# A three-layer graph attention kernel: every product of its loops made at least 65 rows and columns wide, and one tile's weighting moved from GpSimd to VectorE

## What is computed

```python
# layers 0 and 1 (4 heads, then 1), each with a further self loop on every node
xW = x @ W
e = leaky_relu(alpha_s[src] + alpha_d[dst], 0.2)
w = exp(e - segment_max(e, dst)[dst])
out = segment_sum(xW[src] * (w / segment_sum(w, dst)[dst]), dst) + bias
# elu between them; behind layer 1: x = layernorm(x + out)

# layer 2 (8 heads): edge features join the score
enc = relu(edge_attr @ edge_W.T + edge_b)
alpha = (h_src * a_src).sum() + (h_dst * a_dst).sum() + (enc * h_dst).sum()   # per head
# leaky_relu, softmax over the edges of a destination, weighted sum, + bias, residual, layernorm
```

## Time and profile before

| what | value |
|---|---|
| median of 3 runs | 2092.96 us (2092.95 to 2096.61) |
| the profiled execution | 2100.78 us, span 2099.0 us |
| TensorE busy | 1673.1 us, 80% of the span |
| VectorE busy | 1574.9 us, 75% |
| GpSimd busy | 1504.7 us, 72% |
| ScalarE busy | 1370.3 us, 65% |
| mean granted clock of TensorE | 0.824 |

### The profile page before, as it was taken

How to read it: one execution, slowest core, us unless ns; L and a number is a source line. 1 busy time by engine, 2 the same in 40 slices (tenths; PEclk the granted TensorE clock), 3 DMA queues, 4 the chain that set the end, 5 groups by cost and what they waited for, 6 DMA issues and landing times. The chain is left out here.

```text
span 2099.0 us, 43225 instructions
## 1 busy us (share of the span) xinstructions
PE 1673.1 (80%) x9241; PEld 1064.7 (51%) x9241; DVE 1574.9 (75%) x4409; ACT 1370.3 (65%) x5004; POOL 1504.7 (72%) x1648
## 2 busy tenths in 40 slices
PE   7377778777876577878878877789999999999984
PEld 5244445545544344545545444445565655565652
DVE  5567877777778456666656667879899998899997
ACT  3267776777675444545545446668888888888886
POOL 3677777777767577777777773667777777777873
PEclk9578877888787767777777787779999999999995
DMA  7655554555641344444444641434444444444431
GB/s 195 173 161 143 145 143 139 142 144 167 186 116 37 118 129 135 134 129 135 137 129 134 197 121 39 122 109 125 125 129 130 127 130 127 125 128 133 137 90 61
DMA packets 130636, 274.39 MB, mean 131 GB/s; under 512 B 39701, under 2 KB 65274, under 8 KB 130367
## 3 DMA queue, kind: packets, MB, share of 16 engines
q0 software_dynamic: 64128, 181.33, 32.1%
q1 hardware_dynamic: 61564, 86.45, 13.5%
q10 hardware_dynamic: 4699, 3.86, 0.7%
HBM read 255.00 MB, written 17.20 MB: 130 GB/s over the span
## 5 line engine op out<-in xcount | busy, mean ns | idle before, releaser
L1283 POOL DMA_INDIRECT rows<-table,index_all x1100 | 1073.7, 976 | 402.9 <-issue 304.9
L1801 PE MATMUL bank<-rows,onehot 128*128 128x264 f32 (+1 forms) x2200 | 863.2, 492 | 55.0 <-DVE rows L843 17.4
L854 DVE TENSOR_TENSOR sums<-sums,bank 128x264 f32 (+1 forms) x1320 | 556.8, 422 | 325.6 <-PE bank L1801 252.5
L1498 ACT ACTIVATE rows<-rows,wgt 128x33 f32<-128x33 f32 (+2 forms) x2740 | 706.3, 338 | 2.1 <-issue 1.1
L1801 PEld LDWEIGHTS bank<-rows,onehot 128*128 128x128 f32 x2200 | 416.7, 230 | 126.1 <-issue 77.7
L1721 PE MATMUL bank<-identb,onehotT 128*128 128x128 bf16 x1320 | 228.9, 261 | 41.9 <-issue 28.9
L1283 POOL DMA_INDIRECT late<-table,index_all x220 | 214.1, 973 | 67.0 <-issue 62.2
L1721 PEld LDWEIGHTS bank<-identb,onehotT 128*128 128x128 bf16 x1320 | 135.1, 117 | 155.0 <-issue 93.6
L1506 ACT ACTIVATE prod<-bank 128x512 f32<-128x512 f32 x240 | 134.1, 559 | 107.2 <-PE bank L1813 97.0
L1820 PE MATMUL bank<-late,onehotT 128*128 x1320 | 201.0, 290 | 1.3 <-DVE prod L863 1.3
L1450 ACT CAST onehot<-bank 128x768 f32<-128x768 bf16 x240 | 174.5, 729 | 40.5 <-PE bank L1721 40.3
(11 more groups left out here) (215 smaller groups left out, 2242.2 us busy)
## 6 DMA issues: line engine op xcount, KB each, us to landing
locb<-loc_d SPq DMA_DIRECT2D x120, 352.0 KB, 3.8
rows<-table,index_all POOLq DMA_INDIRECT x1100
flags<-flags_d SPq DMA_DIRECT2D x508, 27.5 KB
late<-table,index_all POOLq DMA_INDIRECT x220
table<-rows SPq DMA_DIRECT2D x25, 136.0 KB, 1.8
table<-rows SPq DMA_DIRECT2D x25, 134.0 KB, 2.7
late<-table SPq DMA_DIRECT2D x1, 3300.0 KB
table<-rows SPq DMA_DIRECT2D x25, 129.5 KB, 2.3
```

Of the source, the lines that this page charges most:

```text
L854: done(v.tensor_tensor(a, a, sum_bank(l, t, s)[:, 0:VV], ALU.add), "add")
L1283: g.indirect_dma_start(out=rows_of(l, t)[:, s, 0:ROW[l]], out_offset=None, in_=table[l], in_offset=bass.IndirectOffsetOnAxis(ap=index_all[ ...
L1498: i = a.activation(r, r, ACT.Copy, scale=wgt[:, t.u, h * B + s:h * B + s + 1])
L1801: done(m.matmul(sum_bank(l, t, s)[:, 0:VV], onehot[:, t.u, s, :], rows_of(l, t)[:, s, 0:VV], start=True, stop=True), "agg")
```

## The change

Every product of the loops gets a stationary operand of at least 65 rows and 65 columns. Operands that stood on few partitions (`runs`, `linkrow`, `scale`, `carry`, `edgew3`, `attrT`) get all 128, with zeros, or values that meet zeros, in the added ones. `scoresT`, `weightsT` and the ends' transposes take all 88 lines in each layer. For the ends, `top` is laid out anew, so that 128 columns in a row begin or end at the wanted one; what lies beside it is computed and not used. One wait on the ends of the batch before moves from `tops2` to `tops`. Four buffers are cleared by VectorE at the start, and one more by GpSimd. And in layer 2 tile 4 is multiplied by VectorE in place of GpSimd.

```diff
-OWNER = ("AVAAVAAVAAV", "VAAAAAAAAAA", "VAVAPAPAPAP")
+OWNER = ("AVAAVAAVAAV", "VAAAAAAAAAA", "VAVAVAPAPAP")
...
-        carry = sb("carry", [2, RING, P])
+        carry = sb("carry", [P, RING, P])
...
-        runs = sb("runs", [1, 2, 8 * (B + 1)])
-        linkrow = sb("linkrow", [1, 2, 8 * B])
+        runs = sb("runs", [P, 2, 8 * (B + 1)])
+        linkrow = sb("linkrow", [P, 2, 8 * B])
...
-        scale = sb("scale", [2, 8])
+        scale = sb("scale", [P, 8])
...
-        edgew3 = sb("edgew3", [30, D], BF16)
+        edgew3 = sb("edgew3", [P, D], BF16)
...
-        attrT = lateb[0:30, BLOCKS * 3 * D:].rearrange("p (r f) -> p r f", r=RING)
+        attrT = lateb[:, BLOCKS * 3 * D:].rearrange("p (r f) -> p r f", r=RING)
...
+        LINES = 8 * B
+        ps_leftw = ps_T[:, 256:256 + 8 * (B + 1)].rearrange("p (h s) -> p h s", h=8)
+        ps_rightw = ps_T[:, 352:352 + LINES]
+        LAST, NEXT, FIRST_T = 0, 1, 2
+        topw = top[:, :, :].rearrange("p i e -> p (i e)")
...
+            for unused in (score[:, :, :], expT[:, :, :], top[:, :, :]):
+                ch(v.memset(unused, 0.0))
+            ch(v.memset(edgew3[:, :], 0.0))
...
-                    done(v.tensor_tensor_scan(top[0:R, 1, :], flags[0:R, t.u, PEN_F, :], s0, -BIG,
+                    need(dve, "endp", kk)
+                    done(v.tensor_tensor_scan(top[0:R, NEXT, :], flags[0:R, t.u, PEN_F, :], s0, -BIG,
                                               ALU.add, ALU.max), "topf")
...
                     need(dve, "topf", kk + 1)
-                    need(dve, "endp", kk)
...
-                    sp.dma_start(carry[:, t.u, :], carry_d[...])
+                    sp.dma_start(carry[0:2, t.u, :], carry_d[...])
...
+            g.memset(scale[:, :], 0.0).then_inc(p_zero, 1)
...
+            pool.wait_ge(p_zero, 1)
+            g.memset(scale[0:2, :], 1.0).then_inc(p_pool, 1)
...
-                        r = m.transpose(ps_T[0:H * B, i * P:(i + 1) * P], score[:, i, 0:H * B], ident[:, :])
+                        r = m.transpose(ps_T[0:LINES, i * P:(i + 1) * P], score[:, i, :], ident[:, :])
...
-                    m.matmul(left[:, :, 0], ones[0:1, :], runs[0:1, 0, 0:H * (B + 1)].rearrange(
+                    m.matmul(ps_leftw[:, 0:H, 0], ident[:, :], runs[:, 0, 0:H * (B + 1)].rearrange(
                         "p (h s) -> p h s", h=H)[:, :, B], start=True, stop=True)
-                    m.transpose(left[:, :, 1:], top[0:H * B, 2, P - 1:P],
-                                ident[0:H * B, 0:H * B])
-                    r = m.transpose(ps_right[:, 0:H * B], top[0:H * B, 2, 0:1], ident[0:H * B, 0:H * B])
+                    m.transpose(ps_leftw[:, :, 1:], topw[:, P - 1:2 * P - 1], ident[0:LINES, 0:LINES])
+                    r = m.transpose(ps_rightw, topw[:, 0:P], ident[0:LINES, 0:LINES])
...
-                        r = m.matmul(ps_col[0:H * B, i:i + 1], linkrow[0:1, i, 0:H * B], ones[0:1, :], start=True, stop=True)
+                        r = m.matmul(ps_col[:, i:i + 1], linkrow[:, i, :], ident[:, 0:1], start=True, stop=True)
...
-                    m_ = m.transpose(ps_e[:, WT:WT + H * B], expT[0:H * B, 0, :], ident[0:H * B, 0:H * B])
+                    m_ = m.transpose(ps_e[:, WT:WT + LINES], expT[:, 0, :], ident[0:LINES, 0:LINES])
...
-                        m_ = m.transpose(ps_e[:, QT:QT + H * B], expT[0:H * B, 1, :], ident[0:H * B, 0:H * B])
+                        m_ = m.transpose(ps_e[:, QT:QT + LINES], expT[:, 1, :], ident[0:LINES, 0:LINES])
```

More of the change, by code:

```diff
@@ L317, in gat_kernel @@
         s_bias = sem("s_bias")
-        p_pool, p_dve, p_pe = sem("p_pool"), sem("p_dve"), sem("p_pe")
+        p_pool, p_dve, p_pe, p_zero = sem("p_pool"), sem("p_dve"), sem("p_pe"), sem("p_zero")
         s_dpad = sem("s_dpad")
@@ L769, in tops @@
                     if SELF[l]:
-                        done(v.tensor_tensor(top[0:R, 0, :], s0, scoreT[0:R, 1, :], ALU.max), "top0")
+                        done(v.tensor_tensor(top[0:R, FIRST_T, :], s0, scoreT[0:R, 1, :], ALU.max), "top0")
                         need(dve, "top0", kk + 1)
-                        s0 = top[0:R, 0, :]
-                    done(v.tensor_tensor_scan(top[0:R, 1, :], flags[0:R, t.u, PEN_F, :], s0, -BIG,
+                        s0 = top[0:R, FIRST_T, :]
+                    need(dve, "endp", kk)
+                    done(v.tensor_tensor_scan(top[0:R, NEXT, :], flags[0:R, t.u, PEN_F, :], s0, -BIG,
                                               ALU.add, ALU.max), "topf")
@@ L779, in tops2 @@
                     need(dve, "topf", kk + 1)
-                    need(dve, "endp", kk)
-                    done(v.tensor_tensor_scan(top[0:R, 2, ::-1], flags[0:R, t.u, PEN_B, ::-1], top[0:R, 1, ::-1],
+                    done(v.tensor_tensor_scan(top[0:R, LAST, ::-1], flags[0:R, t.u, PEN_B, ::-1], top[0:R, NEXT, ::-1],
                                               -BIG, ALU.add, ALU.max), "top")
@@ L807, in finish_tops @@
                     done(v.scalar_tensor_tensor(seg[0:R, :], flags[0:R, t.u, PEN_L, :], ps_col[0:R, 0:1],
-                                                top[0:R, 2, :], ALU.add, ALU.max), "seg1")
+                                                top[0:R, LAST, :], ALU.add, ALU.max), "seg1")
                     need(dve, "seg1", kk + 1)
@@ L1128, in meta @@
                     chains(t)
-                    sp.dma_start(carry[:, t.u, :], carry_d[bass.ds(t.k * B, 1), :, :].rearrange("a r e -> (a r) e")).then_inc(s_meta[l][t.u], 16)
+                    sp.dma_start(carry[0:2, t.u, :], carry_d[bass.ds(t.k * B, 1), :, :].rearrange("a r e -> (a r) e")).then_inc(s_meta[l][t.u], 16)
                 def self_rows(l=l):
@@ L1223, in _ @@
             g.memset(carry[:, :, :], 1.0).then_inc(p_pool, 1)
-            g.memset(scale[:, :], 1.0).then_inc(p_pool, 1)
+            pool.wait_ge(p_zero, 1)
+            g.memset(scale[0:2, :], 1.0).then_inc(p_pool, 1)
             g.memset(chain[:, :, :], -BIG).then_inc(p_pool, 1)
@@ L1759, in endsT @@
                     need(pe, "top", kk + 1)
-                    left = ps_left[:, 0:H * (B + 1)].rearrange("p (h s) -> p h s", h=H)
-                    m.matmul(left[:, :, 0], ones[0:1, :], runs[0:1, 0, 0:H * (B + 1)].rearrange(
+                    m.matmul(ps_leftw[:, 0:H, 0], ident[:, :], runs[:, 0, 0:H * (B + 1)].rearrange(
                         "p (h s) -> p h s", h=H)[:, :, B], start=True, stop=True)
-                    m.transpose(left[:, :, 1:], top[0:H * B, 2, P - 1:P],
-                                ident[0:H * B, 0:H * B])
-                    r = m.transpose(ps_right[:, 0:H * B], top[0:H * B, 2, 0:1], ident[0:H * B, 0:H * B])
+                    m.transpose(ps_leftw[:, :, 1:], topw[:, P - 1:2 * P - 1], ident[0:LINES, 0:LINES])
+                    r = m.transpose(ps_rightw, topw[:, 0:P], ident[0:LINES, 0:LINES])
                     done(r, "endp")
```

## The result

The changed kernel took 2069.42 us (median of 4 runs, 2066.95 to 2071.67) beside 2092.95 us for the kernel before on the same chip (4 runs, 2090.33 to 2096.61): a ratio of 0.9883, 95% interval 0.9865 to 0.9901. The profiled execution took 2071.67 us with a span of 2069.9 us, against 2100.78 and 2099.0. One run of all that follow, 2344.9 us at a mean clock of 0.54 in the kernel with only the ends wide, was in a slow state and is left out of that kernel's median.

What follows compares the result with a forecast made beforehand. GpSimd bounds layers 0 and 1; in layer 2 its pace alternates with TensorE delays. Layer 2's batches -33, filling -5, ends -2 make -40 us: 2100.8 to 2060.8, less 7.8 for the profiled execution, 2053 us; range 2038 to 2075.

Steps and rivals of the forecast that it cites:

- the clock still falls: Rival, layer 2: leftover 24-column products or idle time keep the clock falling; 16.5 us a batch, 2070 us; chance 0.22.
- What bounds it, and the clock: GpSimd bounds layers 0 and 1; layer 2 alternates between GpSimd's pace and TensorE delays; narrow products lower the clock.
- Steady batches: Layer 2's loop: 35 batches at 16.15 us each, VectorE the bound, in place of 598 us: -33 us.
- The wide weight loads: Layer 2's loop: ends' transposes and the carried run's product load more columns, costing 0.3 us a batch.
- The switching gain: Layer 2's loop: 0.10 us saved on both sides of six narrow groups, 1.2 us of TensorE time a batch.
- Tile 4 on GpSimd's side: Layer 2: GpSimd loses one 639 ns multiply a batch, going from 16.27 to 15.63 us.
- Layers 0 and 1 themselves: Layers 0 and 1: GpSimd's gathers cover the added TensorE work, so no cost; up to 64 us without cover.
- gathers at another pace: Sign of a wrong forecast: gathers in layers 0 and 1 come at another pace than before.
- Filling and ends: Filling of layer 2 (1344 to 1420 us) gains 5 us; ends of layers 0 and 1 gain 1 us each.
- Start and the moved wait: Start: VectorE's four added clears cost nothing, at most 0.3 us; the wait one scan earlier is met, costing nothing.
- The subtraction for the profiled execution: Whole kernel: the profiled execution stood 7.8 us above the median, so 2060.8 became a forecast of 2053 us.

## Why the prediction was right, and where a step failed

The forecast was 2053 us, the range 2038 to 2075, the measurement 2069.4. The time is that of the rival "the clock still falls" (2070), but not by its way: the clock stands at 1.00, and a batch takes 16.21 us, not 16.5.

- **What bounds it, and the clock: right.** The falls come right behind the narrow work and went when it was widened. They also went when two 128-row products were added ahead of it, so that the narrow products alone don't make a fall. I had named the one- and two-row products, the 30-row pairs and the untouched 24-column products; the runs narrow this to the links' and factor's six instructions, with encode as a helper. The Trainium skill ("TensorE: Matmul & The Clock Gate", Part 1) sets the clock by how busy the engine is and blames idle gaps. The runs here don't bear that out as a full account: 472.5 and 473.7 us busy of 500 went with 0.94 and 1.00, and the 6 us ahead of the falls are as busy in a kernel that has none.
- **Steady batches: right, -31.9 for -33, in part by luck.** 16.15 us was forecast, 16.21 came. VectorE is busy 487.07 / 30.9 = 15.8 us a batch and idle 0.4; I had 15.97 and 0.2, two errors that cancel.
- **The wide weight loads: right in kind.** The ends' four instructions take 0.40 us to the next start (1500.50 to 1500.90), where those before take 0.28 (from 1499.87 to 1500.15 us of its timeline); I allowed 0.3 us a batch.
- **The switching gain: right in size, wrong in use.** The gaps fell by 0.1 us on both sides of a pair, as I read from the earlier trace rows. I counted the 1.2 us a batch as what takes TensorE out of the bound. TensorE is busy 456.0 / 30.9 = 14.8 us a batch where I had 14.5. With the gaps back and the clock up, the batch is the same.
- **Tile 4 on GpSimd's side: mis-sized.** I took 0.64 us off GpSimd. But its three multiplies last 732 ns in the mean, the four had lasted 639, since one of the three is held up beside VectorE's new multiply (last section). By busy time GpSimd saves 4 x 15.1 / 25 - 3 x 65.4 / 93 = 0.31 us. GpSimd's own work and issue are then (399.54 + 89.3) / 30.9 = 15.8 us a batch, not 15.63, level with VectorE. That is one reason why the tile is worth so little.
- **Layers 0 and 1 themselves, 0: the step that failed.** The cover was "GpSimd's gathers". It does hide TensorE's added work: GpSimd's waits for TensorE are 10.7 us there, for 9.7. But the gathers themselves last longer, 983 and 988 ns for 976 and 978, which the prediction had named as a sign of being wrong (gathers at another pace). Layer 0's loop is 2.5 us longer in this pair of profiles and 3.8 us over all, and the kernels with these layers narrow are 6.0 us faster, plus or minus 3.4. How wider products lengthen a gather, the runs don't show; the cause stays open.
- **Filling and ends: mis-sized.** -2.7 us for -5; the kernels with encode at 128 rows fill in 70.7 to 72.2 us, the others in 72.2 to 74.5. The ends gave nothing where I had -2: the passages in which they lie grew by 0.2 and 3.6 us.
- **Start and the moved wait: right.** The first gather starts at 58.3 us (58.4 before); the forward scan (line 783), which now stands behind the wait, is idle 1.1 us in 31 batches.
- **The subtraction for the profiled execution** was 7.8 us, the most of any term that isn't in the kernel. Before's profiled execution lay above the four other runs of its group; the changed kernel's lay only 2.2 above its median. The profiles differ by 29.1 us, the medians by 23.5. Of the 16 us between forecast and measurement, 11 are terms of the sum (-40 against -29.1) and 5.6 are this.

In numbers, the rest of the missing 11 us is: layer 0 and the passage to layer 2, 6.1 where I had nothing (3.6 of it, the passage's, did not come again with the tile back); filling 2.3; ends 2; the steady part 1.1; the other stages gave 0.6.

The experiments show no version that is surely ahead of the one with layers 0 and 1 narrow, 2062.83 us; links and factor alone (2066.33, and 2066.11 with wide transposes in layers 0 and 1) reach the same within their intervals, and of layer 2's products only six a batch need the edit.

## What to carry to other kernels

Where TensorE's clock falls though the engine is busy, list what it did just ahead of the falls by rows used, and widen the products with the fewest rows first: here six one- and two-row instructions a batch held nearly the whole gain. The gains of such edits don't add up: widening encode alone brought 0.51 of the 0.91 us a batch, and beside the six it brought nothing. Widen only in the stage that the falls delay; in layers 0 and 1, bound by GpSimd, the same edit brought nothing and seems to have cost some us. A gap that can be seen on a timeline is only worth something if its engine is the bound: ask what is left of it when the clock is repaired alone.

## What the runs showed of the hardware that was not expected

- **A switch between 64 and 66 rows.** A pair of products of 30 or 64 rows costs 0.1 us more on either side next to 128-row products (0.61 and 0.32 us in place of 0.52 and 0.22); one of 66 rows costs nothing.
- **The clock can stay up with an equally busy engine**: 1.00 at 473.7 us busy of 500, 0.94 at 472.5. In layer 2 the first kernel has the ends', the links' and the factor's products wide and the tile moved; the ends alone give 0.95, the tile alone 0.96. Two 128-row products added ahead of the narrow ones kept it at 1.00 as well, at 470.6 us busy.
- **Operations of GpSimd and VectorE hold each other up.** GpSimd's multiplies last 732 ns in the mean in the changed kernel and 639 with the tile back on GpSimd (734 with the tile moved and nothing widened). The mean hides that one multiply of a batch takes it all: 918 to 933 ns, while the others last 623 to 652. The long one is always the one that starts 9 to 24 ns ahead of VectorE's third multiply, and it ends 492 to 497 ns behind that one's end. The other way round, VectorE's small operation on 8 elements (line 809; line 800 in the kernel before) ends 30 to 36 ns behind the end of the GpSimd multiply that it started beside, in all 91 batches of the changed kernel, the one with the tile back and the kernel before. That is why it lasts 336 ns in the changed kernel and 484 with the tile back, where in 25 of 31 batches it starts earlier beside the multiply; in the kernel before, with the tile on GpSimd too, it lasts 333. One batch of the changed kernel on VectorE's timeline, then GpSimd's second multiply, which runs from 1455.11 us (a window of `--lines` around it):

```profile
1454.87 0.33 DVE L809 TENSOR_TENSOR drop<-runs 1x8 f32<-1x8 f32 x1
1455.12 0.41 DVE L852 TENSOR_TENSOR rows<-rows,wgt 128x264 f32<-128x264 f32 x1
...
L1311 POOL TENSOR_TENSOR rows<-rows,wgt 128x264 f32<-128x264 f32 x1 | 0.9, 919 | 0.0
```

The groups of the kernel with the tile back, 1450 to 1950 us:

```profile
L809 DVE TENSOR_TENSOR drop<-runs 1x8 f32<-1x8 f32 x31 | 15.0, 484 | 2.8
...
L1311 POOL TENSOR_TENSOR rows<-rows,wgt 128x264 f32<-128x264 f32 x124 | 74.8, 639 | 0.5
```

The Trainium skill ("SBUF — State Buffer", section "SBUF: two separate sides") says that VectorE's operations with two inputs in SBUF and GpSimd's share a pair of ports, which one holds for a whole instruction while the other waits. All three operations are of that kind, and the numbers fit: each ends a fixed time behind the other's end. No run here takes the port away, so that the ports are the cause is not shown.
